# Two of four tiles' sums of squares moved from TensorE to VectorE and ScalarE, with two spill buffers, in a block of two layer norms around a masked product and a decoded linear layer

## The reference, cut to what matters

```python
# first half: a masked product of two weights, gelu, residual, layer norm
attn = jnp.einsum('ds,td->st', w1, w2) * sparse_mask
y = jax.nn.gelu(jnp.einsum('bds,st->bdt', x, attn) + b2, approximate=False)
x = _layernorm(x + y)
# second half: weights decoded from bit planes through a table per row
e = jnp.linalg.norm(x, axis=-1)
w_l = dequant_kbit(qweight, lut4, 4)      # 16 values a row
w_h = dequant_kbit(qweight, lut8, 8)      # 256 values a row
y = jnp.where((e > 64.0)[..., None], x @ w_h.T, x @ w_l.T) + bias
x = _layernorm(x + y)
```

## Time and profile before

| | |
|---|---|
| median of three runs | 295.69 us (295.47 to 296.08) |
| the profiled execution | time 296.05 us, span 294.0 us |
| mean granted TensorE clock | 0.99 |
| PE, VectorE, ScalarE, GpSimd busy | 280.9, 221.7, 195.5, 59.6 us |
| matmuls of the linear layer, lines 578, 580, 579 | 424 each; 130.7, 129.9, 129.5 us, overlapping |
| DMA | 49.78 MB, mean 169 GB/s |

### The profile page before, as it was taken

One profiled execution on the slowest core, in us unless ns is written; L12 is line 12 of the kernel. 1 busy time (PEld: TensorE's weight loads), 2 busy tenths in 40 slices (PEclk: granted clock), 3 DMA queues, 4 the chain that ended last, 5 costly groups with the idle time before them and its releaser, 6 DMA issues.

```text
span 294.0 us, 4871 instructions
## 1 busy us (share of the span) xinstructions
PE 280.9 (96%) x1835; PEld 245.1 (83%) x1835; DVE 221.7 (75%) x380; ACT 195.5 (67%) x257; POOL 59.6 (20%) x83
## 2 busy tenths in 40 slices
PE   7799999999999999999999999999999999999990
PEld 3688876676668999999999999999987878887890
DVE  1679999996968977997979686297689778656273
ACT  2766459997999979989989996472457484113110
POOL 4000001533353212421200000001141124262101
PEclk9999999999999999999999999999999999999996
DMA  6999999999999711111111111165088754333423
GB/s 209 398 358 359 376 376 332 255 262 226 206 206 204 148 36 50 42 36 56 36 44 49 38 54 38 55 151 209 25 281 276 258 180 178 113 140 115 175 87 137
DMA packets 28480, 49.78 MB, mean 169 GB/s; under 512 B 2464, under 2 KB 11936, under 8 KB 28448
## 3 DMA queue, kind: packets, MB, share of 16 engines
q1 hardware_dynamic: 23392, 40.53, 40.3%
q0 software_dynamic: 4352, 8.39, 15.8%
q10 hardware_dynamic: 704, 0.46, 0.5%
HBM read 36.79 MB, written 12.58 MB: 168 GB/s over the span
## 4 chain that ended last, share of the span: by engine, by line
PE 66%; ACT 11%; SPq 7%; DVE 6%; issue 4%; DMA 3%; POOLq 0%; POOL 0%; DVEq 0%; ACTq 0%
PE acc L578 17%; PE acc L580 17%; PE acc L579 17%; DMA w<-in_w2d 3%; PE acc L507 3%; ACT leaf L754 3%; ACT zz L797 2%; ACT z L736 2%; SPq L287 2%; PE acc L517 2%; PE acc L482 2%; PE acc L561 1%; DVE zz L1088 1%; SPq L286 1%; SPq L291 1%
## 5 line engine op out<-in xcount | busy, mean ns | idle before, releaser
L578 PE MATMUL acc<-lin,zz 128*128 128x256 f32 (+2 forms) x424 | 130.7, 308 | 0.3 <-issue 0.3
L580 PE MATMUL acc<-lin,zz 128*128 128x256 f32 (+2 forms) x424 | 129.9, 306 | 0.0
L579 PE MATMUL acc<-lin,zz 128*128 128x256 f32 (+2 forms) x424 | 129.5, 305 | 0.0
L578 PEld LDWEIGHTS acc<-lin,zz 128*128 128x128 f32 x424 | 80.1, 189 | 4.5 <-issue 0.5
L580 PEld LDWEIGHTS acc<-lin,zz 128*128 128x128 f32 x424 | 80.0, 189 | 4.1
L579 PEld LDWEIGHTS acc<-lin,zz 128*128 128x128 f32 x424 | 80.2, 189 | 3.9
L754 ACT ACTIVATE leaf<-planes,lut,flip 128x1024 f32<-128x1024 uint8 x56 | 67.6, 1235 | 1.1 <-DVE dest L1046 1.1
L1046 DVE COPY_PREDICATED leaf<-planes,leaf 128x1024 f32<-128x1024 uint8 x32 | 43.5, 1358 | 12.7 <-ACT leaf L754 11.9
L865 ACT ACTIVATE junk<-rows,cols 128x1024 bf16<-128x1024 f32 x15 | 17.2, 1146 | 34.3 <-DVE cols L1172 34.3
L1046 DVE COPY_PREDICATED dest<-planes,leaf 128x1024 f32<-128x1024 uint8 x24 | 32.6, 1358 | 3.6 <-ACT leaf L754 2.3
L1534 POOL DMA_DIRECT2D z<-in_xr x16 | 19.6, 1230 | 69.8 <-ACT z L736 61.8
(11 more groups left out here) (115 smaller groups left out, 408.1 us busy)
## 6 DMA issues: line engine op xcount, KB each, us to landing
z<-in_xt SPq DMA_DIRECT2D x16, 512.0 KB, 9.2
z<-in_xr POOLq DMA_DIRECT2D x16, 512.0 KB, 9.7
out_rows<-rows SPq DMA_DIRECT2D x15, 512.0 KB, 3.2
out_rows<-parts SPq DMA_DIRECT2D x32, 128.0 KB, 1.7
rows<-out_rows SPq DMA_DIRECT2D x16, 256.0 KB, 2.8
w<-in_w1d SPq DMA_DIRECT2D x7, 512.0 KB, 9.1
off_band<-in_mask_rest SPq DMA_DIRECT2D x8, 448.0 KB, 4.7
w<-in_w2d SPq DMA_DIRECT2D x3, 584.0 KB, 9.9
```

The costliest lines, as they stand in the source:

```text
L578: nc.tensor.matmul(bank, hi, w_hi, start=k == 0, stop=False)
L579: nc.tensor.matmul(bank, hi, w_lo, start=False, stop=False)
L580: last = nc.tensor.matmul(bank, lo, w_hi, start=False, stop=k == KB - 1)
```

## The change

- PE makes the squares of tiles 0 and 1 of group 0 only, in banks 4 and 5, both ahead of the first sweep.
- Tiles 2 and 3 of group 0: in the second sweep VectorE adds hi and lo of four blocks, 256 tokens each (`make_first_whole`), ScalarE squares them, VectorE adds them up block by block (`add_first_squares`), twice. PE sums over the partitions by two matmuls behind part 14 of the second sweep (`group_squares(0)`). VectorE copies the two columns next to the other two sums. `square_means()` and `group_variance(0)` stand ahead of `sum_step(1, 0)` and no longer behind the eight sum steps.
- The 8 buffers of the parts become 2 (`SLOTS`). A save waits for the spill of two parts earlier and, in the first sweep, for the mean made from it. The first whole and its sum lie where the six others were; `make_whole(1, 0)` waits for all the spills.
- FIRST_STEPS has two steps less, SECOND_STEPS two more. Turns 2 to 6 come one part later.
- Turn 7 waits for the variance and not for the reads of the squares.
- In the general path PE's code is in loops; some of its semaphores are shared with the main path. `flips_made` becomes a fourth count of `lut_step`.

```diff
-    STATS_AHEAD = 2
-    GRAM_TILES = PER_GROUP
-    SQUARE_BANK = {1: 5, 2: 6, 3: 7}
+    SLOTS = 2
+    GRAM_TILES = 2
+    SQUARE_BANK = (4, 5, 6, 7)
+    FIRST_WHOLE_AT = (4, 9)
+    FIRST_SQUARES_BEHIND = 14
...
-    FIRST_STEPS = [2, 2, 2, 1, 1, 2, 1, 2, 1, 2, 2, 2, 2, 2, 2, 2]
-    SECOND_STEPS = [3, 2, 2, 3, 2, 2, 2, 3, 2, 2, 2, 3, 2, 2, 2, 3]
+    FIRST_STEPS = [2, 2, 2, 1, 1, 1, 1, 1, 2, 2, 2, 2, 2, 2, 2, 1]
+    SECOND_STEPS = [3, 3, 2, 2, 2, 2, 3, 2, 2, 3, 2, 2, 3, 2, 3, 3]
...
-    TURN_IN_FIRST = {6: 2, 12: 3}
-    TURN_IN_SECOND = {1: 4, 6: 5, 11: 6}
+    TURN_IN_FIRST = {7: 2, 13: 3}
+    TURN_IN_SECOND = {2: 4, 7: 5, 12: 6}
...
-        parts = at("parts", 160.25, [8, WIDE], f32)
+        parts = at("parts", 160.25, [SLOTS, WIDE], f32)
+        first_whole = at("first_whole", 162.3125, [HALF_BLOCKS, GROUP // 2], f32)
+        first_square_sum = at("first_square_sum", 166.3125, [GROUP // 2], f32)
...
                 elif b == KB - 1:
-                    pe.wait_ge(squares_read, GRAM_TILES)
+                    pe.wait_ge(var1, 2)
...
             def group_squares(g):
-                pe.wait_ge(squares_added, PAIRS * g)
-                for c in range(PER_GROUP):
...
+                if g == 0:
+                    pe.wait_ge(squares_read, GRAM_TILES)
+                    pe.wait_ge(first_added, KB - 1)
+                    total, first = first_square_sum, GRAM_TILES
+                else:
+                    pe.wait_ge(squares_added, PAIRS * g)
+                    total, first = square_sum, 0
+                for c in range(first, PER_GROUP):
...
-            for j in range(STATS_AHEAD):
+            for j in range(GRAM_TILES):
                 tile_squares(j)
             for j in range(TILES):
-                if STATS_AHEAD <= j + 1 < GRAM_TILES:
-                    tile_squares(j + 1)
                 early_part(0, j)
...
                     turn(TURN_IN_SECOND[j])
+                if j == FIRST_SQUARES_BEHIND:
+                    group_squares(0)
...
             def save(q, j):
                 m = TILES * q + j
                 act.wait_ge(part_done, m + 1)
-                if m >= 8:
-                    act.wait_ge(spilled[m % 8], 16 * (m // 8))
-                    if m < TILES + 8:
-                        act.wait_ge(mean1, m - 7)
+                if m >= SLOTS:
+                    act.wait_ge(spilled[m % SLOTS], 16 * (m // SLOTS))
+                    if m < TILES + SLOTS:
+                        act.wait_ge(mean1, m - SLOTS + 1)
...
                 done = decode_steps(SECOND_STEPS[j], done)
+                if j - 1 in FIRST_WHOLE_AT:
+                    square_whole(0, FIRST_WHOLE_AT.index(j - 1))
                 save(1, j)
...
             def group_variance(g):
                 c = slice(PER_GROUP * g, PER_GROUP * (g + 1))
+                dve.wait_ge(gram_done, GRAM_TILES + g + 1)
+                total = acc[:, SQUARE_BANK[g], 0:PER_GROUP]
                 if g == 0:
-                    dve.wait_ge(squares_read, GRAM_TILES)
+                    nc.vector.tensor_copy(zsq[:, GRAM_TILES:PER_GROUP], total[:, GRAM_TILES:]).then_inc(squares_read, 1)
+                    dve.wait_ge(squares_read, GRAM_TILES + 1)
                     total = zsq[:, c]
...
+            def make_first_whole(r):
+                if r:
+                    dve.wait_ge(first_added, HALF_BLOCKS - 1)
+                blocks, later = slice(HALF_BLOCKS * r, HALF_BLOCKS * (r + 1)), slice(GRAM_TILES * P, GROUP)
+                nc.vector.tensor_tensor(first_whole[:, :, :], zz[:, 0, 0, blocks, later].bitcast(f32),
+                                        zz[:, 1, 0, blocks, later].bitcast(f32), ALU.add).then_inc(whole_made, 1)
+
+            def add_first_squares(r):
+                dve.wait_ge(squared1, r + 1)
+                total = first_square_sum[:, :]
+                for n in range(0 if r else 1, HALF_BLOCKS):
+                    if r or n > 1:
+                        dve.wait_ge(first_added, HALF_BLOCKS * r + n - 1)
+                    so_far = total if r or n > 1 else first_whole[:, 0, :]
+                    nc.vector.tensor_tensor(total, so_far, first_whole[:, n, :], ALU.add).then_inc(first_added, 1)
 
             def make_whole(g, r):
                 if (g, r) == (1, 0):
-                    for slot in range(4):
-                        dve.wait_ge(spilled[slot], 16 * (EARLY_PARTS // 8))
+                    dve.wait_ge(first_added, KB - 1)
+                    for part_spilled in spilled:
+                        dve.wait_ge(part_spilled, 16 * (EARLY_PARTS // SLOTS))
                 if (g, r) == (1, 2):
-                    for slot in range(4, 8):
-                        dve.wait_ge(spilled[slot], 16 * (EARLY_PARTS // 8))
+                    dve.wait_ge(gram_done, GRAM_TILES + 1)
...
             for j in range(TILES):
                 done = decode_steps(SECOND_STEPS[j], done)
+                if j in FIRST_WHOLE_AT:
+                    make_first_whole(FIRST_WHOLE_AT.index(j))
+                if j - 2 in FIRST_WHOLE_AT:
+                    add_first_squares(FIRST_WHOLE_AT.index(j - 2))
+            square_means()
+            group_variance(0)
             sum_step(1, 0)
...
-            square_means()
-            group_variance(0)
```

More of the change, by code:

```diff
@@ L222, in post_ln_block @@
         residual_done = [sem(f"residual_done{r}") for r in range(PAIRS)]
-        warm_made, consts_made, flips_made = (sem(n) for n in ("warm_made", "consts", "flips"))
+        warm_made, consts_made = sem("warm_made"), sem("consts")
         planes_made, leaf_made, merged = sem("planes_made"), sem("leaf_made"), sem("merged")
@@ L565, in tile_squares @@
             def tile_squares(j):
[L566 to L573, removed]
+                cut = slice(j * P, (j + 1) * P)
+                pe.wait_ge(z_lo_made, PAIRS)
+                pe.wait_ge(gelu_done, KB * (GROUPS - 1) + UNIT_BANKS.index(GRAM_BANKS[j]) + 1)
+                squares(GRAM_BANKS[j], lambda k: zz[:, 1, 0, k, cut], lambda k: zz[:, :, 0, k, cut]).then_inc(gram_done, 1)
             def linear(bank, hi_of, lo_of, weights):
@@ L676, in _ @@
                                 g_mixed, 1)
-                def general_pass(before):
+                pe.wait_ge(ones_made, 3)
+                with pe.Fori(0, 2) as n:
+                    with pe.Fori(0, KB) as b:
+                        pe.wait_ge(g_w_ready, KB * n + b + 1)
+                        turn_row(dest[:, 0, :], 5, g_turned)
                     with pe.Fori(0, TILES) as j:
-                        pe.wait_ge(sems["z_lo"], j + (before + 1))
+                        pe.wait_ge(g_lin_lo, KB * n + (KB + 1))
+                        pe.wait_ge(sems["z_lo"], TILES * n + j + 1)
                         squares(GRAM_BANKS[0], lambda k: g_zs[:, 1, k, :], lambda k: g_zs[:, :, k, :])
@@ L686, in general_pass @@
                         last.then_inc(sems["gram"], 1)
[L687 to L701, removed]
+                        with pe.Fori(0, 2) as h:
+                            weights = g_lin[:, bass.ds(h, 1), :, :, :]
+                            linear(acc[:, bass.ds(h, 1), :].rearrange("p a c -> p (a c)"), lambda k: g_zs[:, 1, k, :],
+                                   lambda k: g_zs[:, 0, k, :],
+                                   lambda m, k: weights[:, :, m, k, :].rearrange("p a c -> p (a c)")).then_inc(
+                                       sems["half"], 1)
         @block.scalar
@@ L747, in make_leaf @@
                     if b == 0:
-                        act.wait_ge(flips_made, 1)
+                        act.wait_ge(lut_step, 4)
                     to = dest[:, b % 2, :]
@@ L855, in square_whole @@
             def square_whole(g, r):
-                n = PAIRS * (g - 1) + r
-                act.wait_ge(whole_made, n + 1)
-                part = whole[WHOLE_IN[r]][:, :, :]
+                act.wait_ge(whole_made, PAIRS * (g - 1) + 2 + r + 1 if g else r + 1)
+                part = whole[WHOLE_IN[r]][:, :, :] if g else first_whole[:, :, :]
                 nc.scalar.activation(part, part, ACT.Square).then_inc(squared1, 1)
@@ L1501, in tile_mean1 @@
                 pool.wait_ge(saved, j + 1)
-                nc.gpsimd.tensor_scalar(mean[:, j:j + 1], parts[:, j % 8, QUARTER:QUARTER + 1], 1.0 / D, None,
+                nc.gpsimd.tensor_scalar(mean[:, j:j + 1], parts[:, j % SLOTS, QUARTER:QUARTER + 1], 1.0 / D, None,
                                         ALU.mult).then_inc(mean1, 1)
```

72 lines of the change are left out of this document (37 added, 35 removed).

## The result

| | median, us | runs |
|---|---|---|
| before | 296.08 | 295.47 to 296.75, 5 runs |
| after | 292.18 | 291.83 to 292.41, 5 runs |

The ratio is 0.9867, 95% interval 0.9847 to 0.9888: 3.9 us faster. The forecast was 2.0 us faster, 293.7, with a range from 293.2 to 294.9. The forecast started from a before of 295.69; from the 296.08 of these runs it would have said 294.1, and 1.9 is missing. The profiled execution of after took 291.87 with a span of 290.0.

What follows compares the result with a forecast made beforehand. PE's matmuls were taken as the bound from 92.7 us. Squares -1.90, stall -0.48 and group_squares +0.39 sum to -1.99, so 294.05 us profiled, and with the median 0.36 lower 293.7 us; range 293.2 to 294.9.

Steps and rivals of the forecast that it cites:

- The middle: Stretch from the first record of PE's squares to the last group_squares; forecast to get 1.99 us shorter.
- the squares less `group_squares(0)`: On PE, squares of tiles 2 and 3 go (1.90) and two one-column matmuls come (0.39): 1.51 us gained.
- the lists: Turns 2 to 6 one part later and moved decode steps: PE's stall of 0.48 us at turn 3 goes.
- The deadlines: Claim that decoded weights and z_lo are ready before PE wants them, with margins from 1.0 to 3.3 us.
- z_lo of the last pair: VectorE's rest of z for group 3, first sweep: ends at 127.2, wanted by part 12 at 128.4, margin 1.2.
- block 3: Decoded weights for turn 3 in the first sweep: ready at 132.5, wanted at 134.2, margin 1.7.
- `make_lin_lo(3)`: VectorE's step for the second sweep: ends at 139.9 or sooner, wanted at 140.9, margin 1.0, the smallest.
- the upper bound of VectorE's work: VectorE's added work in the second sweep: 5.3 us, bounds 4.4 to 6.4, covered by idle time, cost nothing.
- The seven additions: VectorE's 128x256 additions in the second sweep: 0.40 each, 2.8 us together, bounds 0.27 and 0.55 each.
- The spill buffers cost nothing: Two buffers at ScalarE's saves: landing and GpSimd's mean fit in two parts, 5.8 us; cost nothing, bounds 0 and 1.0.
- Everything else. PE's loops in the general path ... Nothing.: Loops in PE's general path, flips_made and renamed semaphores: branch not taken or one signal replaced by one, cost nothing.
- the tail: From the last group_squares to the span's end: forecast to gain nothing; prediction fails by size if not just shifted.

Runs made afterwards that it cites:

- experiment 4: The kernel before with only the new lists of steps and turns, all four tiles' squares still on PE: 295.35 us, ratio 0.9973.
- experiment 7: The kernel before with PE waiting for ScalarE's last scaling ahead of its branch over the general path: 296.42 us, ratio 1.0034.
- Experiment 1: The kernel before with only the general path as in the change, PE's code there in loops: 294.67 us, ratio 0.9956.
- Experiment 2: The kernel after with PE's general path written out as before: 293.3 us, ratio 0.9913 to before.
- experiment 6: The kernel after with each make_first_whole done three times, 4.8 us more for VectorE: 294.16 us, ratio 0.9945 to before.
- experiment 10: The kernel after with PE squaring one block of tiles 0 and 1 instead of eight, 14 matmuls less: 293.66 us, ratio 0.9936 to before.
- experiment 3: The kernel after with the old lists of steps and turns: 293.07 us, ratio 0.9905 to before.

## Why the prediction was right in the middle and wrong in size

- **The middle was right**, 2.04 for 1.99, and by its steps: the squares less `group_squares(0)` gave 1.43 for 1.51 and the lists 0.61 for 0.48 (experiment 4 and after). These two errors partly cancel, so that 0.05 is closer than the working was. The windows of after show PE busy for the whole of both sweeps:

```profile
92.40:140.90 48.50, 48.50 (x404) 48.50 (x405) 42.16 (x55) 43.08 (x55) 11.18 (x16) 1.00 0.28 69
140.90:190.00 49.10, 49.10 (x414) 49.10 (x414) 39.92 (x60) 42.14 (x55) 2.18 (x2) 1.00 0.13 44
```

- **The deadlines held.** The timeline of VectorE after:

```profile
125.69 1.22 DVE L1098 TENSOR_TENSOR zz<-z,zz 128x1024 fp32r<-128x1024 f32 x1
131.96 0.42 DVE L1068 TENSOR_TENSOR dest<-dest,eye 128x128 f32<-128x128 f32 x1
138.32 1.22 DVE L1077 TENSOR_TENSOR lin<-acc,lin 128x1024 fp32r<-128x1024 f32 x1
...
172.15 1.23 DVE L1238 TENSOR_TENSOR first_whole<-zz 128x1024 f32<-128x1024 f32 x1
176.19 0.49 DVE L1068 TENSOR_TENSOR dest<-dest,eye 128x128 f32<-128x128 f32 x1
176.55 1.83 DVE L1248 TENSOR_TENSOR first_square_sum<-first_square_sum,first_whole 128x256 f32<-128x256 f32 x4
...
192.37 2.36 DVE L1262 TENSOR_TENSOR whole<-zz 128x1024 f32<-128x1024 f32 x2 [3.47 <-DMA out_rows<-parts]
```

  Forecast and found, as ends: z_lo of the last pair 127.2 and 126.91, block 3 132.5 and 132.38, `make_lin_lo(3)` 139.9 and 139.54, `first_whole` 1 173.5 and 173.38, block 6 176.7 and 176.68, start of `make_whole(1, 0)` 192.8 and 192.37. The walk from durations and overlaps was good to 0.43, and up to 0.34 of a difference is the earlier start. Two sums of the forecast are off by rounding: `make_lin_lo(3)` adds up to 140.0 and not 139.9, and the upper bound of VectorE's work to 6.3 and not 6.4.
- **The seven additions**: four take 1.83, 0.46 each where 0.40 was taken, within the bounds.
- **`group_squares(0)`**: PE's timeline has it as below, 0.36 from its first record to the next part, for the 0.39 of the forecast.

```profile
186.27 0.50 PE L619 MATMUL acc<-cols,first_square_sum 128*128 128x1 f32 x4
186.63 0.37 PE L579 MATMUL acc<-lin,zz 128*128 128x256 f32 x1
```

- **The spill buffers cost nothing**, as taken. The means of GpSimd took 0.2 to 1.95 in after, less than the 3.5 of before, and no save waited for one. The rule of the Trainium skill (SBUF — State Buffer, "Who interferes with whom") may stand behind the spread of the means, which no run here tried. The 5.8 between a save and the next but one was enough for the longest of them, and the trace shows no cost.
- **The step that failed is "Everything else. PE's loops in the general path ... Nothing."** It took code that isn't run for code that costs nothing, and so held the tail for merely shifted, though it named that as the way to fail by size. The loops are worth 1.4 on the kernel before and 1.1 on the kernel after: with the path written out, passing the branch makes the chip fetch a 16 KB packet of PE's code, 2.7 to 3.6 us behind the last matmul in five of six traces, just when the last two stores go out. It lasts 1.0 to 1.4, and the store that ends the kernel lands up to 1.6 later; that it does so by holding one DMA engine is inferred. With the path in loops no packet is fetched there. The Trainium skill (Runtime: NRT & Kernel Launch, "Instruction fetch mechanics") describes such a mechanism: code comes by DMA in blocks of 16 KiB, and a taken branch to code outside of what is held makes a fetch. The trace agrees, with packets of 0.02 MB in q8 that follow the branch in experiment 7 and vanish with the length of the path. Of the rest of 3.9, 2.0 is the middle, and about 0.5 is the scatter of the start and of where before's packet falls.
- **What stays open**: experiments 1 and 2 sum to 1.4 + 2.8 = 4.2 for 3.9, which is within their intervals. Experiment 2 is 0.7 faster than its middle explains. It still has the packet, but starts it with SP's last store (287.17 against an issue at 287.20) and not 0.9 behind it. By the table the place of the packet decides what it costs; what sets that place wasn't tried, nor was the length at which the fetch first comes. Experiment 1 has no q8 packet, and yet its stores take 2.8 and 2.7; an 8 KB packet of another instruction queue, q14, starts 0.6 behind SP's issue there, and whether it is the cause is open.

## What to carry to other kernels

Before calling an unexecuted branch free, ask what lies behind it in the program and what the DMA queues do when it is passed: if the last stores of the kernel are on the way, a code packet among them can cost what it did here, 1.1 to 1.4 us, and a look at the instruction queues in the last 5 us shows it. Idle time of two engines that hand work to each other isn't safe cover for more work: part of it covered the change's own, and none the 4.8 of experiment 6. The margin ahead of each deadline is the safe measure, and there it was used up one for one. Before taking work off the bounding engine, see whether it lies in a wait, for there it costs nothing and may keep the clock up.

## What the runs showed of the hardware

- With one 16 KB instruction packet at the start of two stores of 256 KB these landed in 3.0 to 4.1 us (five traces) instead of 2.0 to 2.8 (seven traces without one); two packets amid them made one store take 4.8.
- After PE had been idle for 2.01 its matmuls started 0.21 apart instead of 0.12 for some 3.2 us (granted clock 0.54 over the 3.6 us window, experiment 10). Idle stretches of 0.64 (experiment 3), 0.56 and 0.97 (experiment 6) left the granted clock at 1.00.
